# Displaced 5x5 depthwise convolution after a group norm: TensorE's loop rotated, fewer waits, a PSUM lane moved to VectorE, and a store issued earlier

## The chip, the cores and the metric

The kernel runs on one core of one Trainium2 chip. The metric is device time in microseconds (us) of one execution; the value of a kernel is the median of several. Besides, one execution was profiled, and all rows below are from that one. TensorE (PE, its weight loads PEld), VectorE (DVE), ScalarE (ACT), GpSimd (POOL) and SyncE (SP) run their own instruction streams and meet at semaphores. A `q` behind an engine's name means its sequencer, which waits, branches and issues DMAs.

## What is computed

The input `x` is float32, 32 x 384 x 64 x 64. It is group-normalised (32 groups of 12 channels), each block of 8 channels is displaced by a whole offset and convolved with a 5x5 Gaussian whose centre is moved by the offset's fraction, and the result is added to `x`:

```python
def _gn(v, G=32, eps=1e-5):
    g = v.reshape(B_, G, C_ // G, H_, W_)
    m = jnp.mean(g, axis=(2, 3, 4), keepdims=True)
    s = jnp.var(g, axis=(2, 3, 4), keepdims=True)
    return ((g - m) / jnp.sqrt(s + eps)).reshape(v.shape)

off_round = jnp.round(offset)                       # offset: 48 positions x (x, y)
disp = _displace(x.reshape(B, P, cpp, h, w), off_int)   # zero outside the image
sub = offset - off_round
d = field[None] + sub[:, None, None, :]
kernel = jnp.exp(-jnp.sum(d * d, axis=-1) / (2.0 * SIGMA ** 2))
kernel = kernel / jnp.sum(kernel, axis=(1, 2), keepdims=True)
out = lax.conv_general_dilated(disp, kw, padding=[(c, c), (c, c)], feature_group_count=C, ...)
x = x + out                                          # of _gn(x)
```

## The kernel before

The convolution is separable, so it is done as two matrix products with band matrices that hold displacement and kernel at once: `ay` for the image's rows and `ax` for its columns.

**Tiles.** The channels are cut into 16 superblocks (`NSUPER`) of 24 channels, the batch into 16 steps (`STEPS`) of two images, which makes 256 steps (`TOTAL`). A step is one slot of `xin`, [128 partitions, 6 channels, 256 elements], 786 KB; there are 16 slots, so each superblock reuses them all. SyncE loads a slot with two DMAs of 384 KB as soon as it has been stored, and ScalarE's sequencer issues the stores, two DMAs each. Four steps make a round (`QUAD`), four rounds a superblock.

**A step on TensorE** has two stages.
- The first stage (`y_product` for three positions, L722 to L729) multiplies the normalised input `norm` with `ay`: 48 products in four row strips of the array. It fills 384 columns of four PSUM banks, `ps[:, v]`. Even steps of a round write half `v` = 0, odd steps half 1. `norm` has two buffers, too, by the step's parity.
- The result is copied from PSUM to `y` (four buffers), one per lane (= bank): `copy_y` on ScalarE (L628), four lanes, and for the last step of a round three lanes, with the fourth copied by VectorE in `copy_last_lane` (L519).
- The second stage (`x_products`, L731) multiplies `y` with `ax` and writes the same PSUM half as the first stage of that parity. VectorE adds two thirds of the result to `xin` (`add_x`, L525); ScalarE copies the other third to `x2` (`copy_third`, L647) and GpSimd adds that (`add_third`, L329). Then the step can be stored.

Between the first stages stand the sums of the group statistics over the partitions, `sum_stats`, 8 small products with `ones`. VectorE makes the statistics themselves (`statistics`, three chunks a step, some five steps ahead), GpSimd turns them into scale and bias (`make_summands`, `coefficients`), and VectorE reads the sums out of PSUM for it (`sums`, L509).

**Normalising** a step is split: half of the channels on ScalarE (L617), half on GpSimd (L334). It can start when the first stage two steps earlier is done (`y_done`), because it overwrites that step's `norm`.

**TensorE's loop** (L825 to L830) runs once a round: an inner loop over the two pairs of `first_stages` (L765), then `second_stages` (L781). The pair before the loop stands apart, so that the inner loop has one pass in the first round. A pair is an even step, `sum_stats`, an odd step. `first_stages` waits before the even step for `x2_ready`, `result1_ready` and `y_ready`, and `y_even` for `norm0_ready`, `half0_ready` and `mats_ready[0]`. Semaphores that TensorE reads count steps, some with a head start of `SPARE` = 2. `second_stages` waits for `ax_ready`, `sums_ready` and the copies of the steps.

**ScalarE's order in a round** (L659 to L701), for steps 0 to 3 of the round: store 0 of the round before, `copy_y` 0, normalise 2, `copy_y` 1, store 1, normalise 3, `copy_y` 2, store 2, `copy_y` 3, store 3, `copy_third` 0, normalise 4, `copy_third` 1, `copy_third` 2, normalise 5, `copy_third` 3. Between superblocks `fill_rows` writes new rows of `ay`. This order is written out by hand, and so are VectorE's (12 statistics, a part of the matrices, `sums`, `copy_last_lane`, four `add_x`) and GpSimd's. A sequencer goes through its instructions in order: what stands behind a DMA issue is not started until the issue is through.

**The first round** of TensorE's loop runs code that is fetched for the first time, and the last four slots (`FIRST` = 12 on) are loaded only after `y_done` has reached 3.

## Time and profile before

| | us |
|---|---|
| median of 3 runs | 1219.58 (1217.87 to 1221.5) |
| the profiled execution, its own time | 1220.7 |
| its span, first to last instruction | 1218.6 |
| TensorE busy | 1157.7 (95%) |
| VectorE busy | 904.9 (74%) |
| GpSimd busy | 823.1 (68%) |
| ScalarE busy | 805.3 (66%) |
| moved between HBM and the core | 402.97 MB |

The span is from the first to the last instruction; the profiled execution's own time is 2.1 us longer. Busy counts neither register, branch and semaphore instructions nor DMA issues. Matmuls overlap in the array, so "busy" on PE is not "at its peak", and a gap on PE or PEld of 0.3 us between two stages is real idle time. In the rows, `[0.60 <-issue]` behind an instruction is the idle time of its engine before it and what ended it; `issue` means nothing that the profile shows. One round of TensorE in the rows is: 96 records of line 726 (a first stage), 8 of line 713 (`sum_stats`), 192 of line 726 (two first stages), 8 of line 713, 96 of line 726, 384 of line 738 (four second stages).

### The profile page before, as it was taken

The numbers are of one execution on the slowest core, as the hardware profiler recorded it, in microseconds if no ns is written. First come the engines' busy times: TensorE is split into PE (matmuls) and PEld (weight loads), VectorE is DVE, ScalarE is ACT, GpSimd is POOL, SyncE is SP. The second block draws the span as 40 slices with busy tenths as digits, with TensorE's granted clock in tenths as the row PEclk, the third lists the DMA queues.
The fourth block names the chain that finished last, engine by engine and source line by source line (L and its number), as shares of the span: only waits on it lengthen the run. The fifth ranks groups of instructions, "written<-read, shape, count | busy, mean of one in ns | idle before, by whom it ended". The sixth has DMA issues, their size and how long they took to land.

```text
span 1218.6 us, 112942 instructions
## 1 busy us (share of the span) xinstructions
PE 1157.7 (95%) x50408; PEld 1127.7 (93%) x50408; DVE 904.9 (74%) x1245; ACT 805.3 (66%) x874; POOL 823.1 (68%) x1176
## 2 busy tenths in 40 slices
PE   7699999999999999999999999999999999999996
PEld 7699999999999999999999999999999999999996
DVE  8467877777877868877777877778778777777762
ACT  4376676666676666676666666666676666676664
POOL 7466766776766866766766766767667666766764
PEclk9899999999999999999999999999999999999999
DMA  9499999999999999999999999999999999999966
GB/s 309 162 320 328 352 342 340 346 345 337 350 340 340 348 341 337 348 341 339 349 346 332 354 337 344 348 341 337 352 338 341 344 341 348 342 342 348 350 221 207
DMA packets 409762, 402.97 MB, mean 331 GB/s; under 512 B 16528, under 2 KB 409744, under 8 KB 409744
## 3 DMA queue, kind: packets, MB, share of 16 engines
q1 hardware_dynamic: 204944, 201.41, 50.2%
q10 hardware_dynamic: 204800, 201.36, 49.6%
q8 instruction: 7, 0.11, 0.0%
q14 instruction: 11, 0.09, 0.0%
HBM read 201.38 MB, written 201.33 MB: 330 GB/s over the span
## 4 chain that ended last, share of the span: by engine, by line
PE 83%; ACT 6%; issue 6%; ACTq 2%; POOL 1%; POOLq 0%; DVE 0%
PE ps L726 60%; PE ps L738 21%; ACT norm L623 4%; PE ps L713 2%; ACT x L651 2%; ACTq L657 2%; ACT ay L612 1%; POOL t_int L245 0%; ACTq L648 0%; POOL grid_i L225 0%; ACTq L650 0%; POOL t_full L252 0%; POOLq L54 0%; POOL grid L239 0%; POOL xin L332 0%
## 5 line engine op out<-in xcount | busy, mean ns | idle before, releaser
L726 PE MATMUL ps<-ay,norm 32*128 32x128 f32 x24576 | 755.9, 274 | 36.1 <-ACT norm L623 28.5
L726 PEld LDWEIGHTS ps<-ay,norm 32*128 32x128 f32 x24576 | 721.8, 188 | 54.2 <-issue 53.6
L634 ACT ACTIVATE y<-ps 128x1536 f32<-128x1536 f32 (+1 forms) x256 | 351.0, 1371 | 296.3 <-PE ps L713 184.8
L498 DVE BATCH_NORM_STATS2 stats<-xin 128x6 f32<-128x512 f32 x768 | 470.8, 691 | 0.1
L738 PE MATMUL ps<-ax,y 64*64 64x64 f32 x24576 | 391.2, 220 | 8.3 <-issue 7.1
L738 PEld LDWEIGHTS ps<-ax,y 64*64 64x64 f32 x24576 | 379.2, 135 | 19.4 <-issue 9.5
L528 DVE TENSOR_TENSOR xin<-ps,xin 128x1024 f32<-128x1024 f32 x256 | 313.5, 1225 | 83.9 <-PE ps L738 83.8
L332 POOL TENSOR_TENSOR xin<-x,xin 128x512 f32<-128x512 f32 x256 | 322.3, 1281 | 12.9 <-ACT x L651 12.6
L341 POOL TENSOR_SCALAR norm<-xin,rstd,bias 128x768 f32<-128x768 f32 x256 | 252.0, 987 | 113.2 <-issue 90.3
L623 ACT ACTIVATE norm<-xin,bias,rstd 128x768 f32<-128x768 f32 x256 | 262.0, 1024 | 23.6 <-issue 13.3
L651 ACT ACTIVATE x<-ps 128x512 f32<-128x512 f32 x256 | 150.7, 589 | 63.0 <-PE ps L738 60.8
L314 POOL TENSOR_TENSOR mean_sq<-both 128x8 f32<-128x8 f32 (+1 forms) x65 | 13.0, 200 | 223.7 <-DVE both L514 221.7
L514 DVE TENSOR_REDUCE both<-ps 128x24 f32<-128x288 f32 x63 | 28.8, 458 | 155.1 <-ACT y L634 155.1
L324 POOL TENSOR_TENSOR rstd<-var,mhalf 128x8 f32<-128x8 f32 (+1 forms) x65 | 106.7, 1642 | 5.1
L521 DVE COPY y<-ps 128x384 f32<-128x384 f32 x64 | 35.7, 558 | 61.5 <-PE ps L726 61.5
L713 PE MATMUL ps<-summands,ones 32*128 32x72 f32 (+1 forms) x1032 | 50.7, 251 | 1.2 <-POOL summands L295 1.2
L713 PEld LDWEIGHTS ps<-summands,ones 32*128 32x128 f32 x1032 | 45.2, 189 | 2.0 <-issue 0.9
L612 ACT ACTIVATE ay<-t_msk,same 128x256 f32<-128x256 f32 x48 | 23.7, 533 | 13.6 <-issue 11.6
L295 POOL TENSOR_TENSOR summands<-stats 128x24 f32<-128x24 f32 (+1 forms) x65 | 22.3, 343 | 9.8 <-POOL summands L293 9.7
L483 DVE SCALAR_TENSOR_TENSOR t_msk<-t_isq,t_exp 128x960 f32<-128x960 f32 x16 | 18.4, 1151 | 0.0
L460 DVE TENSOR_TENSOR t_full<-t_int,sub 128x960 f32<-128x960 f32 x15 | 17.8, 1186 | 0.0
L321 POOL TENSOR_TENSOR var<-spread,mean_sq 128x8 f32<-128x8 f32 (+1 forms) x65 | 14.0, 215 | 5.2 <-POOL spread L319 0.2
(63 smaller groups left out, 211.8 us busy)
## 6 DMA issues: line engine op xcount, KB each, us to landing
xin<-in_x_dram SPq DMA_DIRECT2D x512, 384.0 KB, 5.5
out_dram<-xin ACTq DMA_DIRECT2D x512, 384.0 KB, 5.3
off<-in_L_conv_offset_dram SPq DMA_DIRECT2D x1, 48.0 KB, 3.2
```

The source lines that it names most:

```text
L324: pool.tensor_tensor(rstd[:, v, part], var[:, v, part], mhalf[:, part], ALU.pow).then_inc(small, 1)
L332: pool.tensor_tensor(at, x2[:, s % QUAD], at, ALU.add).then_inc(result0_ready, 1)
L341: pool.tensor_scalar(norm[:, s % 2, :, cols].rearrange("p r (q w) -> p q r w", w=HW), xin[:, s, QG:].rearrange("p q (r w) -> p q r w", w=H ...
L498: nc.vector.bn_stats(stats[:, s // QUAD % 2, s % QUAD, n, :], xin[:, s].rearrange("p (g q) f -> p q f g", g=GROUPS)[:, n]).then_inc(bn_don ...
L528: nc.vector.tensor_tensor(at, ps[:, s % 2, 0:2].rearrange("p h (k f) -> p h k f", k=2), at, ALU.add).then_inc(result1_ready, 1)
L612: filled_k = nc.scalar.activation(ay[:, k].rearrange("p r (m b) -> p (r m) b", b=B)[:, :, part], t_msk[:, k, 0:R].rearrange("p r m -> p (r ...
L623: nc.scalar.activation(norm[:, s % 2, :, cols].rearrange("p r (q w) -> p q r w", w=HW), xin[:, s, 0:QG].rearrange("p q (r w) -> p q r w", ...
L634: nc.scalar.activation(y[:, j].rearrange("p k r a m -> p a (k r) m")[:, 0:lanes], ps[:, j % 2, 0:lanes, 0:POS * P].rearrange("p a (n m) -> ...
L651: nc.scalar.activation(x2[:, s % QUAD], ps[:, s % 2, 2:4, 0:ROW], ACT.Copy).then_inc(x2_ready, 1)
L713: last = nc.tensor.matmul(ps[:, v, a, place], ones[rows, :], summands[rows, part].rearrange("p t n s -> p (t n s)"), start=True, stop=True)
L726: last = nc.tensor.matmul(ps[:, v, a, P * k:P * (k + 1)], norm[rows, v, r, P * k:P * (k + 1)], ay[rows, k, r, :], start=(r == 0), stop=(r ...
L738: last = nc.tensor.matmul(ps[outs, v, 2 * (k // 2) + h, at:at + HW], y[rows, j, k, r].rearrange("p a m -> p (a m)")[:, outs], ax[rows, k], ...
```

## The change

- `second_stages` of a round comes first in TensorE's loop, then the first stages of the next round. The first stages of steps 2 and 3 stand before the loop. In the last pass the inner loop still makes one pair of first stages, for steps that don't exist; ScalarE and GpSimd raise the semaphores for it at their ends.
- Waits go: `y_ready` before both stages of a pair, `half0_ready` and `mats_ready[0]` before an even step, `ax_ready` and `y_ready` before the second stages. ScalarE waits for `half0_ready` at a superblock's border instead.
- VectorE copies the fourth lane of steps 0 and 1 of a round, too, between its statistics (after 3 and after 7 of the 12), and ScalarE's copies of those steps have three lanes. ScalarE waits for VectorE's copy before it normalises steps 2 and 3.
- Statistics run 17 chunks ahead, not 15, and `sums` stands before the making of the matrices.
- On ScalarE the store of step 3 of the round before is issued before `copy_y` 3, not behind it; `copy_third` 1 comes before normalise 4, and `copy_third` 2 before the second part of `fill_rows`.
- Slots 12 to 15 are first loaded when `x_done` has reached 4.

```diff
-AHEAD = QUAD + 1
+AHEAD = 17
...
-                    sync.wait_ge(y_done, 3)
+                    sync.wait_ge(x_done, ADDS * PAIR)
...
+            pool.engine_nop().then_inc(norm1_ready, PAIR)
+            pool.wait_ge(mats_ready[POS - 1], TOTAL)
+            pool.engine_nop().then_inc(mats_ready[POS - 1], 1)
...
-                dve.wait_ge(y_ready, evicted + 1 + SPARE)
+                dve.wait_ge(y_ready, evicted + 1)
...
-            def copy_last_lane(t):
+            def copy_last_lane(t, j):
+
                 dve.wait_ge(y_done, t + 1)
-                nc.vector.tensor_copy(y[:, QUAD - 1].rearrange("p k r a m -> p a (k r) m")[:, LANES - 1],
-                                      ps[:, 1, LANES - 1, 0:POS * P].rearrange("p (n m) -> p n m", m=32)
-                                      ).then_inc(last_lane_ready, QUAD)
+                nc.vector.tensor_copy(y[:, j].rearrange("p k r a m -> p a (k r) m")[:, LANES - 1],
+                                      ps[:, j % 2, LANES - 1, 0:POS * P].rearrange("p (n m) -> p n m", m=32)
+                                      ).then_inc(last_lane_ready, 1 + j // (QUAD - 1))
...
-            nc.vector.engine_nop().then_inc(y_ready, SPARE)
...
+            for part in range(AHEAD - CHUNKS * (QUAD + 1)):
+                statistics(0, QUAD + 1, part)
...
-                for f in range(s + AHEAD, s + AHEAD + QUAD):
+                for m in range(QUAD * CHUNKS):
+
+                    if m == 3:
+                        copy_last_lane(t, 0)
+                    if m == 7:
+                        copy_last_lane(t + 1, 1)
+                    f, part = divmod(CHUNKS * s + AHEAD + m, CHUNKS)
                     if f >= STEPS and not group_follows:
                         continue
...
-                    all_statistics(c + f // STEPS, f % STEPS)
+                    statistics(c + f // STEPS, f % STEPS, part)
+                if last:
+
+                    dve.wait_ge(y_ready, t + 3)
+                    nc.vector.engine_nop().then_inc(sums_ready, QUAD)
+                else:
+                    sums(quad + 1, (g + 1) % 2, t + 2, read=not first)
...
-                copy_last_lane(t + 3)
+                copy_last_lane(t + 3, QUAD - 1)
...
                 act.wait_ge(made, c + 1)
+                if k == 0:
+
+                    act.wait_ge(half0_ready, STEPS * (c + 1))
...
-                lanes = LANES - j // (QUAD - 1)
+                lanes = LANES if j == 2 else LANES - 1
...
                 copy_y(t, 0, first)
+                act.wait_ge(last_lane_ready, t + 1)
                 normalise(t + 2, s + 2, quad, first)
                 copy_y(t + 1, 1, first)
                 store_of_last_round(1)
+                act.wait_ge(last_lane_ready, t + 2)
                 normalise(t + 3, s + 3, quad, first)
                 copy_y(t + 2, 2, first)
                 store_of_last_round(2)
+                store_of_last_round(3)
                 copy_y(t + 3, 3, first)
-                store_of_last_round(3)
...
                 copy_third(t, s, first)
+                copy_third(t + 1, s + 1, first)
                 if not last:
                     normalise(t + 4, (s + 4) % STEPS, quad + 1)
-                copy_third(t + 1, s + 1, first)
+                copy_third(t + 2, s + 2, first)
                 if border:
                     fill_rows(c + 1, 1)
-                copy_third(t + 2, s + 2, first)
...
+            act.wait_ge(norm0_ready, TOTAL)
+            act.sem_inc(norm0_ready, PAIR)
+            act.wait_ge(mats_ready[1], TOTAL)
+            act.sem_inc(mats_ready[1], 1)
...
                 pe.wait_ge(norm0_ready, number)
-                pe.wait_ge(half0_ready, number)
-                pe.wait_ge(mats_ready[0], number)
                 y_product(0, 0)
...
-                after = pe.snap(number + 1)
                 pe.wait_ge(x2_ready, one)
                 pe.wait_ge(result1_ready, one)
-                pe.wait_ge(y_ready, number)
                 y_even(number)
                 pe.wait_ge(summands_ready, number)
                 sum_stats(0)
-                second = pe.snap(one + 1)
+                second, after = pe.snap(one + 1), pe.snap(number + 1)
                 pe.wait_ge(x2_ready, second)
                 pe.wait_ge(result1_ready, second)
-                pe.wait_ge(y_ready, after)
                 y_odd(after)
...
             def second_stages(one):
-                pe.wait_ge(ax_ready, one)
+
+
                 pe.wait_ge(sums_ready, one)
-                pe.wait_ge(y_ready, pe.snap(one + 4))
                 pe.sem_inc(x_started, 1)
                 x_products(0)
-                pe.wait_ge(last_lane_ready, one)
-                pe.wait_ge(y_ready, pe.snap(one + 5))
+                three = pe.snap(one + 3)
+                pe.wait_ge(last_lane_ready, three)
+                pe.wait_ge(y_ready, three)
...
-            begin = pe.alloc_register("begin")
-            pe.reg_mov(begin, 1 + PAIR)
+            y_even(3)
+            pe.wait_ge(summands_ready, 3)
+            sum_stats(0)
+            y_odd(4)
             with pe.Fori(1, TOTAL + 1, QUAD) as one:
-                end = pe.snap(one + QUAD)
-                with pe.Fori(begin, end, PAIR) as number:
-                    first_stages(one, number)
-                pe.reg_mov(begin, end)
                 second_stages(one)
+
+                following = pe.snap(one + QUAD)
+                end = pe.alloc_register("end")
+                pe.reg_alu(end, pe.snap(one + 2 * QUAD), TOTAL + 1 + PAIR, ALU.min)
+                with pe.Fori(following, end, PAIR) as number:
+                    first_stages(following, number)
```

## Rows read from the trace of the kernel before

**Rows 1.** The page: busy us of each engine; what the DMA queues moved.
```profile
PE 1157.7 (95%) x50408; PEld 1127.7 (93%) x50408; DVE 904.9 (74%) x1245; ACT 805.3 (66%) x874; POOL 823.1 (68%) x1176
...
DMA packets 409762, 402.97 MB, mean 331 GB/s; under 512 B 16528, under 2 KB 409744, under 8 KB 409744
```

**Rows 2.** Timeline of PE: start us, us, what, count [idle before], second and last rounds.
```profile
72.29 2.96 PE L726 MATMUL ps<-ay,norm 32*128 32x128 f32 x96 [0.46 <-ACT norm L623]
...
1190.80 2.96 PE L726 MATMUL ps<-ay,norm 32*128 32x128 f32 x96 [0.49 <-ACT norm L623]
...
1202.56 5.87 PE L738 MATMUL ps<-ax,y 64*64 64x64 f32 x384
```

**Rows 3.** Timeline of all engines, one round, from its second first stage on.
```profile
627.10 1.02 ACT L623 ACTIVATE norm<-xin,bias,rstd 128x768 f32<-128x768 f32 x1
...
628.44 2.80 PEld L726 LDWEIGHTS ps<-ay,norm 32*128 32x128 f32 x96 [0.29 <-issue]
628.48 1.45 ACT L634 ACTIVATE y<-ps 128x1536 f32<-128x1536 f32 x1 [0.36 <-PE ps L726]
...
628.69 1.39 ACTq L657 DMA_DIRECT2D out_dram<-xin  x2
...
630.18 1.03 ACT L623 ACTIVATE norm<-xin,bias,rstd 128x768 f32<-128x768 f32 x1 [0.25 <-issue]
...
631.34 2.81 PEld L726 LDWEIGHTS ps<-ay,norm 32*128 32x128 f32 x96
...
631.75 1.45 ACT L634 ACTIVATE y<-ps 128x1536 f32<-128x1536 f32 x1 [0.54 <-PE ps L713]
631.96 1.39 ACTq L657 DMA_DIRECT2D out_dram<-xin  x2
...
634.27 5.95 PE L738 MATMUL ps<-ax,y 64*64 64x64 f32 x371
...
634.48 1.13 ACT L634 ACTIVATE y<-ps 128x1152 f32<-128x1152 f32 x1 [1.28 <-PE ps L726]
...
634.68 1.50 ACTq L657 DMA_DIRECT2D out_dram<-xin  x2
...
636.34 0.60 ACT L651 ACTIVATE x<-ps 128x512 f32<-128x512 f32 x1 [0.74 <-PE ps L738]
```

**Rows 4.** Timeline of PEld: the first weight load of the next round.
```profile
640.85 1.33 PEld L726 LDWEIGHTS ps<-ay,norm 32*128 32x128 f32 x42 [0.60 <-issue]
```

**Rows 5.** TensorE's sequencer before it: duration ns min/median/max, first and last start us.
```profile
L825 PEldq ALU_OP  x1: 32/32/32, 640.0 to 640.0; - x1
L825 PEldq COMPARE_BRANCH  x1: 214/214/214, 640.1 to 640.1; - x1
...
L745 PEldq EVENT_SEMAPHORE  x1: 51/51/51, 640.5 to 640.5; - x1
```

**Rows 6.** Groups by line and shape: busy us, mean ns of one, idle before.
```profile
L498 DVE BATCH_NORM_STATS2 stats<-xin 128x6 f32<-128x512 f32 x768 | 470.8, 691 | 0.1
...
L634 ACT ACTIVATE y<-ps 128x1152 f32<-128x1152 f32 x64 | 72.3, 1130 | 83.3 <-PE ps L726 83.3
...
L521 DVE COPY y<-ps 128x384 f32<-128x384 f32 x64 | 35.7, 558 | 61.5 <-PE ps L726 61.5
```

**Rows 7.** Store issues at the end, columns as rows 5: the third, the other five.
```profile
L657 ACTq DMA_DIRECT2D out_dram<-xin x1: 608/608/608, 1208.6 to 1208.6; - x1
...
L657 ACTq DMA_DIRECT2D out_dram<-xin x5: 1022/1046/1117, 1209.2 to 1213.7; - x5
```

**Rows 8.** Windows: busy us by engine (PE, PEld, DVE, ACT, POOL), PEclk, DMA, GB/s.
```profile
622.48:640.88 18.40, 17.78 (x784) 17.39 (x785) 14.28 (x20) 11.91 (x14) 13.58 (x20) 1.00 1.03 344
...
1209.00:1218.60 9.60, 0.00 (x0) 0.00 (x0) 0.24 (x1) 0.13 (x1) 1.29 (x2) 0.71 0.91 308
```

**Rows 9.** Timeline of the first round's second stages and the next round's begin.
```profile
42.77 3.37 PE L738 MATMUL ps<-ax,y 64*64 64x64 f32 x127 [3.89 <-issue]
...
52.38 4.59 PE L726 MATMUL ps<-ay,norm 32*128 32x128 f32 x96 [0.56 <-issue]
```

More of the change, by code:

```diff
@@ L570, in one_round @@
                         values(c + 1)
-                if last:
-                    nc.vector.engine_nop().then_inc(sums_ready, QUAD)
-                else:
-                    sums(quad + 1, (g + 1) % 2, t + 2, read=not first)
-                copy_last_lane(t + 3)
+                copy_last_lane(t + 3, QUAD - 1)
                 if g == ROUNDS - 1 and group_follows:
@@ L796, in second_stages @@
                 x_products(2)
-                three = pe.snap(one + 3)
                 pe.wait_ge(x2_ready, three)
```

2 lines of the change are left out of this document (1 added, 1 removed).

## Prediction

> **What bounds the kernel now.** I read the page's busy shares first. TensorE is busy for 1157.7 of 1218.6 us and no other engine for more than 905 [rows 1], so the time is TensorE's order of work plus its gaps. Next the period. From the round at 72.29 to the one at 1190.80 us there are 61 rounds, so one takes 18.34 us [rows 2]. There are 63 such rounds after the slow first one, and whatever is won or lost in a round counts 63 times. Then one round in order of time [rows 3]: two pairs of first stages, then four second stages. The gaps sit at the joints. TensorE's weight loads stand idle for 0.29 us before the second pair begins at 628.44, and for 0.60 us between the second stages and the next round [rows 3, 4]. Within the second stages 5.95 us stand for 384 matmuls, against 5.87 in the last round, where nothing follows [rows 2, 3].
>
> Last, the chain through ScalarE, whose sequencer issues the stores between the instructions that TensorE needs. The copy of step 1's result starts at 628.48. Its store issue runs from 628.69 to 630.08, the normalising that waits behind it starts at 630.18 and ends at 631.21, and TensorE begins step 3 at 631.34, 0.13 later [rows 3]. The copy of step 3 runs from 634.48 to 635.61, and since the second stage of step 1 writes the same PSUM half, it cannot start before. The second stage of step 0 started at 634.27 and needs about 5.87/4 = 1.47 us, so it is done at 635.74. That copy is on time by 0.1 us and no more.
>
> **The change part by part.** A round is taken as its times in rows 3, and each part shifts them.
>
> *Order and length of the PE loop.* The order of the matmuls is the same: what was done at the loop's head is done before the loop for steps 2 and 3, and at its foot for the next round. What moves is the loop's own instructions. Before, the joint from second to first stages holds add, branch, two register operations and three waits: from the add at 640.0 to the first weight load at 640.85, of which the branch and what follows it take 0.3 us [rows 4, 5]. After, the branch lies behind first stages, where the sequencer runs ahead (there the weight loads begin 0.29 late only because of ScalarE, or at once). In its place come one or two additions and a minimum, some 0.1 us each by the spacing of those rows, and two of the three semaphore instructions go. 0.85 becomes about 0.55, a gain of 0.30 us (bounds 0.15 and 0.45). At the joint from first to second stages the branch costs 0 to 0.1; I take 0.03 and count it in the 0.30.
>
> *First pair to second pair.* VectorE takes a lane of step 0, so ScalarE's copy falls from 1.45 to 1.13 us [rows 3, 6], and the normalising that ended at 628.12 ends at 627.80. TensorE came 0.32 after it, behind two more semaphore instructions that go away. Both together exceed the gap, so the 0.29 us is gone: the second pair starts at 628.15. The new wait stands on ScalarE, ahead of the normalising, and behind it queue everything of the round. It is met: VectorE's lane takes 0.56 us against 1.13 of ScalarE's [rows 6], if it begins with it. VectorE has three statistics of 0.69 us before it [rows 6] and the whole first stage of step 0 for them, 2.96 us [rows 2], since the copy starts only when that is through. If it came late, each 0.1 us beyond the slack of 0.57 (1.13 less 0.56) would be lost in every round.
>
> *Second pair, step 3.* Here the gain is lost again. The normalising for step 3 started 1.70 us after the copy did, because 1.39 us of store issue lie between, not because of the copy, which ended at 629.93. The copy of step 1 waits for step 1, which has not moved. So step 3 begins at about 631.34 as before, and so does the second stage of step 0 at 634.27. VectorE's second lane buys nothing.
>
> *The store of step 3 ahead of the copy of step 3.* This decides. The copy of step 2 starts 0.29 earlier, at 631.46. Its store's issue ends 1.60 us after (631.75 to 633.35 now), at 633.06. The next store starts 0.21 later, at 633.27, takes D, and then about 0.2 us to the copy's start (its own wait is long met): 633.47 + D, against 634.48. The copy is late by D - 1.01, and it was just in time, so the second stages wait for all of it. For D the nearest rows are: 1.39 us for a pair of issues with room before it, 1.50 for this store now, though it follows the last by 1.33 us [rows 3]. When stores follow each other at once, at the kernel's end, the third issue took 0.61 and the fourth to eighth 1.02 to 1.12 us each [rows 7]. A pair that stands third and fourth would be 0.61 + 0.16 + 1.02 = 1.79. I take D = 1.60, between 1.50 and 1.79, since four issues in a row are only just the number at which it began. So +0.59 us a round; bounds +0.38 (D = 1.39) and +1.09 (D = 2.10, both issues near 1.0).
>
> The Trainium skill (Perfetto Trace Analysis, DMA Instruction — HWDGE) says that an issue's profiled time includes waiting for a descriptor generator that another sequencer may hold locked. By it one load issue in the way would add some 0.6 us, so D would be 2.0 and the kernel near 1261 us. The trace neither shows nor excludes it.
>
> *Copies of the third rows.* The copy at 636.34 started only when the store's issue had ended at 636.18 [rows 3]; that store is now elsewhere, and the copy of step 1 no longer stands behind a normalising of 1.03 us. This takes the second stages from 5.95 to about 5.87 us and something more in the border rounds: 0.10 us a round (0.05 to 0.20). The normalising moved back is due 2 us later, so nothing is late for it.
>
> *VectorE's order.* Two copies of 0.56 us a round are added to 14.28 busy of 18.40 [rows 8], with room. The statistics go two chunks further ahead before the loop, which hides them. The distances and values now stand behind the sums; nothing on the path asks for them.
>
> *Head.* The first pass through new code stalls TensorE, once for 3.89 us [rows 9], while the loads of the last four slots are in flight. They now start after two second stages, which takes away up to 3 us. Steps 2 and 3 have code of their own now, so the loop's first stages are fetched later, for one to two more stalls of up to 3. I take +0.5 (bounds -3 and +6).
>
> *Tail.* The loop now ends with one pair of first stages on no data, and their release is ScalarE's, behind its last store issue, which starts at 1213.7 and takes 1.12 [rows 7]: 1214.8. TensorE has then been idle for 6 us and its clock is down: 0.71 granted on average over the last 9.6 us, so part of it at 1.2 GHz [rows 8]. A first stage at such a start took 4.59 us against 2.96 [rows 2, 9]. So 1214.9 + 4.6 + 0.2 + 2.9 = 1222.6, and 0.4 to the end, against 1218.6: +4.5 us (2.8 at full clock, 7 if both steps are slow).
>
> **The sum.** 0.59 - 0.30 - 0.10 = +0.19 us a round, times 63 = +12.0; with the head 0.5 and the tail 4.5, +17 us. The profiled execution took 1220.7 us (span 1218.6 and 2.1 around it): 1237.7. It stands 1.1 above the median of 1219.58, so 1236.6, and I say 1236.
>
> **The rivals.**
> - *The gains and the late copy cancel* (0.18). D stays at 1.39 to 1.45, since the store issue of this kernel seldom backs up while the loads share the engines. Then -0.02 to +0.04 a round, and with the tail 1216 to 1225. For it: most pairs of issues are 1.39. Against: the tail's fourth issue.
> - *Back-pressure* (0.13). D reaches 2.1: 1.09 - 0.40 = +0.69 a round, 43 us, near 1265; above D of about 1.8 the kernel leaves my case.
> - *Faster* (0.14). The copy of step 3 isn't late, because the two stores' issues are through before step 3 ends or my spacing between them is too wide, while every shorter joint holds: 0.30 + 0.10 + 0.29 = 0.69 us a round, 43 us, less the tail: near 1182. It needs step 3 to begin 0.29 earlier too, and the row of the store issue before its normalising speaks against that. With only the joint and the thirds won it is 0.40 x 63 - 5 = 20 us, near 1200. The point from which it decides: a copy that starts later than 634.3 in this round's time undoes it. The Trainium skill (SBUF — State Buffer, A bandwidth-pool intuition that's wrong) gives about 358 GB/s between HBM and one core. The trace moves 344 over a round [rows 8], and 402.97 MB in 64 rounds at 358 would hold a round at 17.6 us, which is where this rival ends, so it would not go below.
> - *The change doesn't do what it says* (0.05). The removed waits were merged into instructions that remain, so the joints stay as long as they are, and only the late copy counts: 0.59 x 63 + 5 = 42, near 1262.
>
> **How the numbers follow.** My case has 0.50 and spreads over D from 1.45 to 1.8 and the joint's bounds: 1222 to 1252. Faster by over 0.3% (below 1216): 0.14 and a third of the cancelling case, 0.20. Within 0.3%, which is about what a measurement of this kernel can tell from no change: most of the rest of that case and the low edge of mine, 0.15. Slower: 0.65. The range is 1204 to 1258: it leaves out most of the faster case and the top of the back-pressure.
>
> **What would show it.** Right: ScalarE's queue shows four issues in a row of 3.2 to 3.4 us in each round, the copy of 128x1152 starts right behind them, and TensorE waits inside the second stages for that copy, 0.5 to 0.7 us a round, as a new row of the waits. The joint to the first stages falls from 0.60 to about 0.3, the one between the pairs vanishes, step 3's normalising still ends 2.7 us after the copy starts, and the round is 18.5 us. At the end stand 192 matmuls of first stages from 1.2 GHz on. Wrong: a copy that starts within 0.1 us of step 3's end, or a pair of issues that stays at 1.39.

## The result, and the profile after

The changed kernel takes 1247.48 us (median of 4 runs, 1246.37 to 1250.61), against 1219.55 us for the kernel before (median of 4 runs) on the same chip: the ratio is 1.0233, with a 95% interval of 1.0208 to 1.0258. It is slower by 27.9 us; 16.5 were forecast. The profiled execution has a span of 1244.5 us and its own time is 1246.4.

The page of the kernel after: engine shares, bandwidth, and two waits out of its list.

```profile
PE 1155.9 (93%) x50608; PEld 1130.8 (91%) x50608; DVE 968.7 (78%) x1373; ACT 750.7 (60%) x874; POOL 853.0 (69%) x1176
...
HBM read 201.38 MB, written 201.33 MB: 324 GB/s over the span
...
PEld ps L762 <- issue: 77.0, 94, 4.4
...
ACT y L651 <- PE ps L762: 156.9, 53, 3.6
```

Against [rows 1] TensorE does 192 matmuls more (the pair on no data) and is busy for 1.8 us less, while the span is 25.9 us longer. So the loss is idle time. The new waits are on the second stages, now line 762: their weight loads stand idle 94 times for 77 us in total. "Issue" means that the profile shows no releaser, so the cause has to be read from the order of events. First the period: these two rows answer [rows 2].

```profile
70.39 2.38 PE L750 MATMUL ps<-ay,norm 32*128 32x128 f32 x73
...
1212.62 2.96 PE L750 MATMUL ps<-ay,norm 32*128 32x128 f32 x96
```

There are 61 rounds between them, so a round takes 18.73 us, where it took 18.34. (The row at 72.29 in [rows 2] and the one at 70.39 here begin the third of the 64 rounds, not the second, which begins at 52.38 [rows 9].) One round in order of time, TensorE and ScalarE, which answers [rows 3]. Line 750 is a first stage, 737 the sums, 762 a second stage, 651 `copy_y`, 640 the normalising, 668 `copy_third`, 674 a store's issue.

```profile
640.96 1.13 ACT L651 ACTIVATE y<-ps 128x1152 f32<-128x1152 f32 x1 [0.68 <-PE ps L750]
641.07 0.54 DVE L526 COPY y<-ps 128x384 f32<-128x384 f32 x1
641.17 1.39 ACTq L674 DMA_DIRECT2D out_dram<-xin  x2
...
642.68 1.03 ACT L640 ACTIVATE norm<-xin,bias,rstd 128x768 f32<-128x768 f32 x1 [0.59 <-issue]
...
643.76 2.96 PE L750 MATMUL ps<-ay,norm 32*128 32x128 f32 x96
643.82 1.45 ACT L651 ACTIVATE y<-ps 128x1536 f32<-128x1536 f32 x1
644.02 4.12 ACTq L674 DMA_DIRECT2D out_dram<-xin  x4
...
646.74 1.63 PE L762 MATMUL ps<-ax,y 64*64 64x64 f32 x96
...
648.33 1.13 ACT L651 ACTIVATE y<-ps 128x1152 f32<-128x1152 f32 x1 [3.06 <-PE ps L762]
...
649.56 4.43 PE L762 MATMUL ps<-ax,y 64*64 64x64 f32 x288 [1.20 <-issue]
...
653.92 2.96 PE L750 MATMUL ps<-ay,norm 32*128 32x128 f32 x96
```

Four store issues in a row last from 644.02 to 648.14. The copy of step 3 starts behind them at 648.33, though TensorE had finished step 3 at about 646.7. It ends at 649.46, and 0.10 later TensorE goes on, having been idle for 1.20 us. This is the step that the prediction called decisive. Its size is different: 4.12 us for the four issues, where 3.2 to 3.4 were forecast (on average over the rounds they take 4.02). The profile names "PE ps L762" as what the copy waited for. That is only the semaphore that came last; what held it was its own sequencer.

Two other places are as described or better. The second stages go over to the next round at 653.92 with no idle time in brackets (0.60 before, [rows 4]), and between the pairs nothing is idle any more. Step 3 still waits for a normalising that stands behind a store issue (642.68 to 643.71, TensorE at 643.76).

The end of the kernel, TensorE and ScalarE's queue:

```profile
1230.55 6.21 ACTq L674 DMA_DIRECT2D out_dram<-xin  x6
...
1236.96 4.30 PE L750 MATMUL ps<-ay,norm 32*128 32x128 f32 x96 [6.60 <-ACTq L724]
1241.08 0.36 PE L737 MATMUL ps<-summands,ones 32*128 32x72 f32 x8
1241.26 2.91 PE L750 MATMUL ps<-ay,norm 32*128 32x128 f32 x96
```

The pair on no data starts when ScalarE's last six issues are through. TensorE had been idle for 6.60 us by then and the first step takes 4.30 us instead of 2.96. The window of these stages (us, busy time of PE, PEld, DVE, ACT, POOL, granted clock, DMA share, GB/s) has a granted clock of 0.74, so part of it ran at 1.2 GHz:

```profile
1235.00:1244.40 9.40, 7.21 (x200) 7.05 (x200) 0.00 (x0) 0.00 (x0) 0.00 (x0) 0.74 0.49 167
```

To compare kernels I took from each trace the mean distance between the first weight loads of successive stages, over the 62 rounds from the third on. S0 to S3 are the first stages, X0 to X3 the second stages of a round. The row "by matmuls" has the distance from S3 to X0 between their first matmuls instead. D is the time from the start of the first to the end of the second issue of the store of step 3, over the rounds in which loads still run (the stores of rounds 3 to 58).

```
us              before  after    E1    E2    E4    E5    E6    E8    E7   E10   E12
S0 to S1          2.90   2.90  2.90  2.90  2.90  2.90  2.90  2.90  2.90  2.90  2.90
S1 to S2          3.04   2.68  2.69  3.04  3.06  2.68  2.68  2.84  2.69  2.79  2.68
S2 to S3          2.93   3.14  3.15  2.90  2.90  3.13  3.14  2.98  2.91  2.95  3.06
S3 to X0          2.92   2.91  2.91  2.92  3.12  2.91  2.92  2.91  2.93  2.91  2.92
  by matmuls      2.87   3.07  3.08  2.86  3.09  3.05  3.06  3.14  2.98  3.03  3.00
X0 to X1          1.41   2.69  1.54  2.68  1.40  1.88  1.98  1.61  1.48  1.54  1.51
X1 to X2          1.53   1.39  1.55  1.39  1.46  1.39  1.40  1.56  1.93  1.40  1.40
X2 to X3          1.50   1.40  1.40  1.41  1.42  1.40  1.40  1.40  1.39  1.44  1.42
last load of X3
 to next S0       0.70   0.20  0.20  0.69  0.37  0.20  0.20  0.20  0.20  0.20  0.20
round            18.34  18.73 17.75 19.34 18.02 17.89 18.01 17.80 17.83 17.52 17.48
D                 1.51   2.32  1.67  2.04  1.54  1.48  1.61  1.76  2.13  1.42  1.41
```

The two rows for S3 to X0 differ in the kernels with the rotated loop. In the kernel after, in E1 and in E10 the first weight load of X0 is issued in time, but the second follows only 0.17 to 0.18 us later, and with it the first matmul (0.04 in E4, 0.01 in the kernel before). Two lines of E1:

```profile
614.63 0.13 PEld L762 LDWEIGHTS ps<-ax,y 64*64 64x64 f32 x1
614.92 5.69 PEld L762 LDWEIGHTS ps<-ax,y 64*64 64x64 f32 x383 [0.16 <-issue]
```

So about 0.2 us a round that belongs to the joint from first to second stages stands in the row X0 to X1 (in E4 in S3 to X0).

### The profile page after: what moved, and what is told of

Read it like the earlier page. It is cut to its first block and busy times, and to the rows that moved or that the text cites. A ratio compares the mean times of both kernels' runs of the same rounds, so it can differ in the third digit from the quotient of the medians.

```text
span 1244.5 us, 113105 instructions
## 1 busy us (share of the span) xinstructions
PE 1155.9 (93%) x50608; PEld 1130.8 (91%) x50608; DVE 968.7 (78%) x1373; ACT 750.7 (60%) x874; POOL 853.0 (69%) x1176
## 5 line engine op out<-in xcount | busy, mean ns | idle before, releaser
L651 ACT ACTIVATE y<-ps 128x1152 f32<-128x1152 f32 (+1 forms) x256 | 310.1, 1211 | 349.5 <-PE ps L762 156.9
L502 DVE BATCH_NORM_STATS2 stats<-xin 128x6 f32<-128x512 f32 x768 | 482.5, 693 | 0.0
L762 PEld LDWEIGHTS ps<-ax,y 64*64 64x64 f32 x24576 | 379.2, 135 | 84.6 <-issue 77.0
L762 PE MATMUL ps<-ax,y 64*64 64x64 f32 x24576 | 388.3, 219 | 72.2 <-issue 69.0
L314 POOL TENSOR_TENSOR mean_sq<-both 128x8 f32<-128x8 f32 (+1 forms) x65 | 50.9, 784 | 207.9 <-DVE both L518 205.9
L526 DVE COPY y<-ps 128x384 f32<-128x384 f32 x192 | 106.2, 553 | 65.1 <-PE ps L737 40.6
L737 PE MATMUL ps<-summands,ones 32*128 32x72 f32 (+1 forms) x1040 | 47.8, 250 | 1.0 <-POOL summands L295 1.0
L295 POOL TENSOR_TENSOR summands<-stats 128x24 f32<-128x24 f32 (+1 forms) x65 | 15.0, 230 | 9.8 <-POOL summands L293 9.7
L319 POOL TENSOR_TENSOR spread<-inner,both 128x8 f32<-128x8 f32 (+1 forms) x65 | 13.8, 213 | 5.4
```

The costliest lines, as they stand in the source:

```text
L502: nc.vector.bn_stats(stats[:, s // QUAD % 2, s % QUAD, n, :], xin[:, s].rearrange("p (g q) f -> p q f g", g=GROUPS)[:, n]).then_inc(bn_don ...
L526: nc.vector.tensor_copy(y[:, j].rearrange("p k r a m -> p a (k r) m")[:, LANES - 1], ps[:, j % 2, LANES - 1, 0:POS * P].rearrange("p (n m) ...
L651: nc.scalar.activation(y[:, j].rearrange("p k r a m -> p a (k r) m")[:, 0:lanes], ps[:, j % 2, 0:lanes, 0:POS * P].rearrange("p a (n m) -> ...
L737: last = nc.tensor.matmul(ps[:, v, a, place], ones[rows, :], summands[rows, part].rearrange("p t n s -> p (t n s)"), start=True, stop=True)
L762: last = nc.tensor.matmul(ps[outs, v, 2 * (k // 2) + h, at:at + HW], y[rows, j, k, r].rearrange("p a m -> p (a m)")[:, outs], ax[rows, k], ...
```

## The experiments

The theory after the result: the store of step 3 ahead of the copy costs more than everything else gains, and apart from it the change makes the kernel faster. The rivals: the new waits and lanes cost the time, or the gains are limited by the transfers anyway.

**E1, the store behind the copy again.** All of the change but this:

```diff
                 store_of_last_round(2)
-                store_of_last_round(3)
                 copy_y(t + 3, 3, first)
+                store_of_last_round(3)
```

> The changed kernel, but the store of step 3 is issued behind the copy of step 3 again, as in the kernel before. Theory (the two store issues in a row hold that copy back, 2.69 us between the second stages of steps 0 and 1 where 1.40 are needed): that gap falls to 1.40, all other joints stay as in the changed kernel, so the round is 18.73 - 1.29 = 17.44 us and the time 1247.5 - 62 x 1.29 = about 1167 us. Rival (the transfers bind as soon as TensorE's order doesn't: the rate over a round would have to be 361 GB/s, and the highest of the page's slices after the change are 350): the round stays near 18.0 us, 1247.5 - 62 x 0.73 = about 1202 us, and TensorE or VectorE shows waits for loads or stores. Rival (the joint itself is slower, not the copy): no change from 1247 us.

Measured: 1186.96 us, ratio to before 0.9733 (0.971 to 0.9757). So one line in the order turns a loss of 2.3% into a gain of 2.7%; its own share is 60.5 us, 0.98 us a round. The round of 17.75 us lies between the 17.44 of the theory and the 18.0 of the rival: the forecast of 1167 was too good. The copies of the thirds stand behind a store issue again (X1 to X2 1.55 for 1.39), and X0 to X1 is 1.54, not 1.40. The trace of E1, from the copy of step 3 on:

```profile
632.41 1.13 ACT L651 ACTIVATE y<-ps 128x1152 f32<-128x1152 f32 x1 [1.50 <-PE ps L750]
632.43 5.83 PE L762 MATMUL ps<-ax,y 64*64 64x64 f32 x384
632.60 1.60 ACTq L674 DMA_DIRECT2D out_dram<-xin  x2
```

The copy starts with the second stages, and these run through: 5.83 us for 384 matmuls. The 1.55 us from X1 to X2 are a mean: in the rounds before a superblock's border it is 1.80 us, because `fill_rows` stands there as well, and in some others the store's issue is longer (D goes up to 2.28). The 1.54 from X0 to X1 are not the copy's: in every round it starts 0.08 to 0.21 us behind the first weight load of X0, as in the kernel before (0.13 to 0.21). They are the late second weight load shown above; between first matmuls X0 to X1 is 1.41 us.

**E2, the move of the store alone**, in the kernel before, the same two lines:

> The kernel before with one part of the change: the store of step 3 is issued ahead of the copy of step 3. Theory: the pair of issues takes 2.3 us as in the changed kernel, the copy starts 1.60 + 0.21 + 2.3 + 0.2 = 4.3 us after the copy of step 2 where it started 2.75 after, so 1.55 us late; some 0.15 comes back from the thirds; 1.4 x 62 = 87 us slower, about 1306 us. Rival (the long issues come from the shorter round, more bytes a us, and not from four issues in a row): the pair stays near 1.6, the copy is 0.85 late, 0.7 x 62 = 43 us, about 1263 us.

Measured: 1286.54 us, ratio 1.056 (1.0538 to 1.0581). D is 2.04 us and X0 to X1 2.68, and the round is 19.34. With E1 this shows the mechanism from both sides. The forecast of 1306 took D from the kernel after (2.32) and was too high; the result lies halfway between it and the rival's 1263. So both have a part in the long pair of the kernel after: the four issues in a row (1.51 to 2.04 with nothing else changed) and the rest of the change, with its shorter round (2.04 to 2.32). One round of E2:

```profile
641.03 1.45 ACT L634 ACTIVATE y<-ps 128x1536 f32<-128x1536 f32 x1 [0.48 <-PE ps L713]
641.22 3.72 ACTq L657 DMA_DIRECT2D out_dram<-xin  x4
645.10 1.13 ACT L634 ACTIVATE y<-ps 128x1152 f32<-128x1152 f32 x1 [2.62 <-PE ps L738]
```

**E4, the rotated loop alone**, in the kernel before, with the pair on no data and all waits kept:

```diff
-            begin = pe.alloc_register("begin")
-            pe.reg_mov(begin, 1 + PAIR)
+            first_stages(1, 3)
             with pe.Fori(1, TOTAL + 1, QUAD) as one:
-                end = pe.snap(one + QUAD)
-                with pe.Fori(begin, end, PAIR) as number:
-                    first_stages(one, number)
-                pe.reg_mov(begin, end)
                 second_stages(one)
+
+                following = pe.snap(one + QUAD)
+                end = pe.alloc_register("end")
+                pe.reg_alu(end, pe.snap(one + 2 * QUAD), TOTAL + 1 + PAIR, ALU.min)
+                with pe.Fori(following, end, PAIR) as number:
+                    first_stages(following, number)
```

> The kernel before with the rotated loop of TensorE alone, extra pair at the end included; all waits stay, no lane moves, the stores stay. Theory (the branch and the loop's registers are what the joint from second to first stages is made of): 0.70 us from the last weight load of a round to the next falls to about 0.40; 0.3 x 62 = 19 us less, 4 us more at the end, about 1205 us. Rival (the joint is made of waits): it stays near 0.65, and with the end 1219 to 1223 us. In both the joint between the two pairs stays at 3.04 us, since it hangs on ScalarE's copy and normalising.

Measured: 1204.58 us, ratio 0.9888 (0.9866 to 0.991). The time is the expected one, but it comes about otherwise. The joint to the first stages falls from 0.70 to 0.37, as expected, and 0.20 of that is lost at the other joint, where the branch now stands (S3 to X0 is 3.12 us for 2.92 by weight loads, 3.09 for 2.87 by matmuls). What makes up for it is 0.15 from X1 to X3, perhaps because the second stages start later against ScalarE's order and find more of its copies done; that isn't shown. The kernel after doesn't have the kept waits, and its joints are 0.20 by weight loads and 3.07 by matmuls. So the removed waits bring about another 0.17 at the joint to the first stages and next to nothing at the other. No run takes out the waits alone.

**E5 and E6, why the issues last so long.** Both are the changed kernel with one thing left out, so that their output isn't the asked one. E5 leaves out the loads of superblocks 2 to 16; the statistics wait for the store of the slot instead. E6 keeps every load and its number of pieces, but each piece is a quarter as wide. E6's edit:

```diff
-            def load(c, s):
+            THIN = ROW // 4
+
+            def load(c, s, wide=ROW):
                 for b in range(B):
-                    sync.dma_start(xin[b:P:B, s], x_t[s, b, c]).then_inc(loaded[s], 16)
+                    sync.dma_start(xin[b:P:B, s, :, 0:wide], x_t[s, b, c][:, :, 0:wide]).then_inc(loaded[s], 16)
...
                 for s in range(SLOTS):
                     sync.wait_ge(stored[s], 16 * B * c)
-                    load(c, s)
+                    load(c, s, THIN)
```

> The changed kernel without the loads of superblocks 2 to 16: every slot is loaded once, the rest computes on what lies there, and VectorE's statistics wait for the store of the slot instead of its load. It leaves out 189 MB of loads. Theory A (a store issue is long when ScalarE's own queue is full, and loads matter only as they slow its draining): the pair of the store of step 3 stays long, 1.8 us or more as in the kernel's end, the gap between the second stages of steps 0 and 1 at 2.1 or more, the time above 1210 us. Theory B (issues hold each other up, the generator is shared with SyncE's loads): with no loads issued the pair falls to 1.39, the gap to 1.75, the round to 17.8 and the time to 1190 us or less.

> The changed kernel with loads of a quarter of the width from superblock 2 on: as many load issues with as many pieces (384 of 256 B instead of 1024 B), 25% of the bytes; the other three quarters of a slot keep what was there. Theory (a store issue is long when the queue of stores drains slowly beside the loads' bytes): the pair of the store of step 3 falls from 2.32 us to 1.5, as without loads, the gap between the second stages of steps 0 and 1 from 2.69 to about 1.9, the time to about 1200 us. Rival (the load issues themselves are in the way): pair and gap stay, 1240 us or more.

Measured: E5 1196.21 us, ratio 0.9825 (0.9804 to 0.9845), with D at 1.48. E6 1204.46 us, ratio 0.9873 (0.9856 to 0.9891), with D at 1.61. The four issues of one round in E5 and in E6:

```profile
632.78 3.12 ACTq L673 DMA_DIRECT2D out_dram<-xin  x4
```

```profile
637.97 3.13 ACTq L676 DMA_DIRECT2D out_dram<-xin  x4
```

E5 comes out near the numbers of theory B (pair 1.39, round 17.8, 1190 us) and far from those of theory A, but E6 speaks against B's reason: with as many load issues as before but a quarter of their bytes, most of the excess is gone. So what makes a store issue long here is the loads' bytes under way, and not the number of load issues beside it. The last rounds of the kernel after say the same with nothing left out. Its last load issue is at 1180 us; from then on the four store issues of a round take 3.12 to 3.13 us, about as in E5 (3.14 on average), against 4.02 on average in the rounds before:

```profile
1186.14 3.12 ACTq L674 DMA_DIRECT2D out_dram<-xin  x4
```

The total is the same although there the two issues of a store follow each other at 0.03 us (D is 1.74 then) and in E5 at 0.16 us (D is 1.48). So D alone depends on the spacing, too, and the length of all four is the better measure.

I counted the store issues of the kernel after between 100 and 1150 us by how many store issues had started in the 3.2 us before each, and by whether a load issue ran at the same time. With none or one before it, an issue beside a load issue takes 0.62 to 0.63 us on average (120 of them, at most 0.75); the median of all its store issues is 0.62. With two before it, the 101 issues beside which no load issue ran take 0.78 on average and up to 1.30, and in E5 none of that kind takes more than 0.65. With three before it, 49 ran beside a load issue and take 1.25 on average, at most 2.05; the 6 others take 0.95. In E5 the fourth of a row takes 0.72 us on average. The prediction weighed the rule of the Trainium skill (Perfetto Trace Analysis, DMA Instruction — HWDGE) that an issue also waits for a generator which another sequencer holds. By it D would have been 2.0, near the measured 2.32. But a load issue beside a lone store issue doesn't lengthen it, and store issues get long with no load issue beside them, so that rule alone doesn't explain the excess. 1.25 against 0.95 for the fourth leaves room for a share of it, but a long issue also has more time to meet a load issue.

What E5 and E6 don't tell is whether the issue waits for the queue's own earlier stores or for room that all queues share. The kernel after had both, four stores in a row and the loads beside them.

**E8, VectorE's new lanes left out of E1.** ScalarE copies four lanes of steps 0 and 1 again.

```diff
-                lanes = LANES if j == 2 else LANES - 1
+                lanes = LANES - j // (QUAD - 1)
...
-                    if m == 3:
-                        copy_last_lane(t, 0)
-                    if m == 7:
-                        copy_last_lane(t + 1, 1)
...
-                act.wait_ge(last_lane_ready, t + 1)
...
-                act.wait_ge(last_lane_ready, t + 2)
```

> The run with the store of step 3 behind the copy, without VectorE's copies of a lane of steps 0 and 1 (ScalarE copies all four, 1.45 us). Theory (since TensorE comes 0.05 us after what it waits for, where it was 0.33 before, the waits taken out were worth about as much as the lane): step 1 to step 2 is 0.33 + 1.35 + 1.02 + 0.05 = 2.75 us instead of 2.69, step 3 doesn't move as it hangs on the store issue; 0 to 0.1 us a round, 1187 to 1193 us. Rival (the lane made the gain, as I had it in the prediction): 3.0 us, 0.3 x 62 = 19 us, about 1206 us.

Measured: 1190.61 us, ratio 0.9761 (0.9742 to 0.9781), against 0.9733 for E1: the lanes are worth about 0.05 us a round (17.80 for 17.75), and the intervals overlap. S1 to S2 is longer without them (2.84 for 2.69) and S2 to S3 shorter by about as much (2.98 for 3.15). What VectorE's lane gives to step 2, the store issue ahead of the normalising takes from step 3.

**E7, E10, E11 and E12, the other stores.** If a store issue ahead of work that TensorE needs costs time, the others do too. E7 is E1 with the store of step 1 behind the normalising of step 3:

```diff
-                store_of_last_round(1)
                 act.wait_ge(last_lane_ready, t + 2)
                 normalise(t + 3, s + 3, quad, first)
+                store_of_last_round(1)
```

> The run with the store of step 3 behind the copy, and the store of step 1 behind the normalising of step 3, too. Theory (ScalarE's queue sets the start of step 3: 1.70 us from the copy of step 1 to the normalising, of which the copy needs 1.13): step 2 to step 3 falls from 3.15 to 2.90 us, the round from 17.75 to 17.50, 0.25 x 62 = 15 us less, about 1171 us, at 360 GB/s over a round. Rival (the transfers are the bound from about 355 GB/s on): the gain is given back by waits for stores or longer issues, 1180 to 1187 us.

Measured: 1192.21 us, ratio 0.9762 (0.974 to 0.9783), no better than E1. S2 to S3 falls from 3.15 to 2.91, as meant, and X1 to X2 rises from 1.55 to 1.93:

```profile
633.94 1.54 ACTq L674 DMA_DIRECT2D out_dram<-xin  x2
...
636.67 2.55 ACTq L674 DMA_DIRECT2D out_dram<-xin  x2
...
639.38 1.08 ACT L668 ACTIVATE x<-ps 128x512 f32<-128x512 f32 x2 [1.77 <-PE ps L762]
...
640.12 3.03 PE L762 MATMUL ps<-ax,y 64*64 64x64 f32 x192 [0.67 <-ACT x L668]
```

Three stores now stand close together, the last pair takes 2.55 us, and the copies of the thirds behind it come late. The lateness has moved to another place. The rival named longer issues, too, but ascribed them to a bound of the transfers from about 355 GB/s on; E10, below, averages 358 and is faster.

E10 is E7 with the store of step 3 behind the first copy of a third, and with ScalarE's releases for the pair on no data ahead of the last three stores:

```diff
                 copy_y(t + 3, 3, first)
-                store_of_last_round(3)
...
                 copy_third(t, s, first)
+                store_of_last_round(3)
                 copy_third(t + 1, s + 1, first)
...
                 if last:
+                    act.wait_ge(norm0_ready, TOTAL)
+                    act.sem_inc(norm0_ready, PAIR)
+                    act.wait_ge(mats_ready[1], TOTAL)
+                    act.sem_inc(mats_ready[1], 1)
                     for j in range(1, QUAD):
                         store(c, s + j, t + j)
             run(one_round)
...
-            act.wait_ge(norm0_ready, TOTAL)
-            act.sem_inc(norm0_ready, PAIR)
-            act.wait_ge(mats_ready[1], TOTAL)
-            act.sem_inc(mats_ready[1], 1)
```

> The store of step 1 behind the normalising of step 3, the store of step 3 behind the first copy of thirds, and at the end ScalarE raises the semaphores of the extra pair before its last three stores. Theory: as the run with the store of step 1 moved (about 1171 us), and the border rounds lose their 0.3 us before the second stage of step 2 (16 x 0.3 = 5 us less); at the end TensorE's extra pair runs beside the stores, so that from the last second stage to the end it is 10.4 us as before the change instead of 14.4: about 1162 us. Rival (transfers bound): 1175 us and more, with the end still 4 us shorter.

Measured: 1167.57 us, ratio 0.9569 (0.9552 to 0.9586). The round is 17.52 us, and from the last load of the second stages to the end it takes 10.45 us instead of 14.4, so the tail's 4 us are gone as well. Rows of E10's end, and three windows, two of one round each and one of 1000 us (us, then busy time of PE, PEld, DVE, ACT, POOL, granted clock, DMA share, GB/s):

```profile
1155.59 1.17 PE L749 MATMUL ps<-ay,norm 32*128 32x128 f32 x32 [0.30 <-ACTq L720]
1155.67 6.03 ACTq L674 DMA_DIRECT2D out_dram<-xin  x6
```

```profile
629.73:647.10 17.37, 17.21 (x791) 17.08 (x785) 14.23 (x21) 11.56 (x14) 12.97 (x18) 1.00 1.05 354
647.10:664.50 17.40, 17.30 (x794) 17.17 (x788) 15.55 (x23) 12.20 (x16) 12.23 (x19) 1.00 1.07 365
...
100.00:1100.00 1000.00, 989.22 (x44732) 978.51 (x44725) 855.69 (x1197) 666.14 (x771) 751.26 (x1015) 1.00 1.06 358
```

TensorE is busy for 17.21 of 17.37 us of a round: here it is the bound. The transfers run at 358 GB/s on average, 343 in the same window of the kernel before, and no engine's waits name a load of `xin`: so the rival that they limit the gains isn't borne out up to this rate. What is left stands in the first round of a superblock, which takes 17.96 us against 17.37 in the others. Two more runs tried small things on E10: E11 loads slots 12 to 15 already when `y_done` is 3, as the kernel before does, and E12 puts the store of step 0 behind the normalising of step 2 in those first rounds.

```diff
-                    sync.wait_ge(x_done, ADDS * PAIR)
+                    sync.wait_ge(y_done, 3)
```

> The fastest run so far (stores of steps 1 and 3 moved, the extra pair released earlier) with the last four slots loaded from y_done 3 on, as in the kernel before. Theory (the loads delay the fetch of code that TensorE runs for the first time): the first round's stall in the second stages grows again by some 2 to 3 us, the second round begins at 71 to 72 us instead of 69.3, the time is 2 to 3 us longer. Rival (the later loads bring nothing, the other parts of the change shorten the head): no change.

```diff
-                store_of_last_round(0)
+                if g:
+                    store_of_last_round(0)
                 copy_y(t, 0, first)
                 act.wait_ge(last_lane_ready, t + 1)
                 normalise(t + 2, s + 2, quad, first)
+                if not g:
+                    store_of_last_round(0)
```

> The fastest run so far, with the store of step 0 behind the normalising of step 2 in the first round of each superblock. There ScalarE's copy of step 0 waits 0.7 us behind a store that waits for GpSimd's addition, and the joints into steps 2 and 3 are 0.47 and 0.18 longer than in the other rounds. Theory: these rounds fall from 17.96 to about 17.4 us, 15 x 0.55 = 8 us less, about 1159 us. Rival (the store only moves its lateness, to the stores that follow or to VectorE's waits for a free slot): 1165 us or more.

Measured: E11 1166.71 us, ratio 0.9572 (0.9557 to 0.9587); E12 1167.22 us, ratio 0.9577 (0.9561 to 0.9592). Neither differs from E10. When the last slots are loaded doesn't matter: the delay that E11's theory forecast for the head isn't there. In E12, S1 to S2 of the first rounds falls from 3.15 to 2.68 us and S2 to S3 rises from 3.08 to 3.55, so those rounds stay at 17.96: the lateness moved once more. The trace shows where to. The list of waits of E12 has this row:

```profile
PEld ps L739 <- POOL summands L295: 7.3, 16, 0.6
```

Line 739 is `sum_stats`, which stands between S2 and S3. In all 15 such rounds of E10 and of E12 it begins 0.05 us behind GpSimd's `summands`, where these are ready 0.58 us before it in the other rounds. So there GpSimd's queue holds TensorE, and a store moved on ScalarE can't help. No run changes GpSimd's order, so what that would bring is open. The best versions, E10 to E12, are 4.3% faster than the kernel before and about 6.5% faster than the changed one.

## Why the prediction was right, and where its terms were off

The direction, the place and the order of size were right: the late copy outweighs the gains. The sum came out lower than the measurement by 11 us, out of errors that partly cancel, and that the time lies in the range is in part luck. With the measured D and the forecast gains, the prediction's own sum gives 0.91 us a round and about 1282 us, outside the range. The gains were 0.89 us a round instead of 0.40.

```
us a round                          forecast   measured
last second stage to first stages     -0.30      -0.50   (0.70 to 0.20)
step 1 to step 3                       0         -0.15   (5.97 to 5.82)
late copy of step 3 (X0 to X1)        +0.59      +1.28   (1.41 to 2.69)
copies of the thirds (X1 to X3)       -0.10      -0.24   (3.03 to 2.79)
sum                                   +0.19      +0.39   (18.34 to 18.73)
```

Over 61 rounds the measured sum is 23.7 us. The head gives 1.9 back (the third round starts at 70.39 instead of 72.26 us), and the tail costs 4.0 (14.4 us from the last load of the second stages to the end, 10.4 before): together 25.8, against 25.9 between the spans.

- **The late copy: the mechanism right, D mis-sized.** D was taken as 1.60 and is 2.32 us. The prediction read it from the kernel's end [rows 7], where the third and fourth issues took 0.61 and 1.02. In the rounds of the kernel after they take 0.95 and 1.21 on average. Part of the error was the row: at the end no loads are under way, and E5 and E6 show that loads with their bytes are what lengthens the issues. The other part was the choice of a value below what the row gave: it gave 1.79, and the kernel after has 1.74 in its last rounds, without loads. By its own formula, D - 1.01, the delay would have been 1.31 with the right D, and the measured rise of X0 to X1 is 1.28. D belongs to the back-pressure rival, which gave 2.1 and 1265 us (its own terms, 43 us for the rounds and 5 for head and tail, make 1268); the kernel isn't that slow because the gains were larger than forecast.
- **The joint to the first stages: half as much again.** 0.50 us went, where the bounds were 0.15 and 0.45. In the trace one addition, one register move and one semaphore instruction are left in the place of [rows 5]: they start at 653.5, 653.7 and 653.8, and the weight load at 653.92. The addition begins while the last second stage still runs, and the branch is no longer there. E4 shows that the rotation alone brings 0.33 at this joint and loses 0.20 at the other; the rest at this joint, 0.17, came with the waits gone. The prediction put the branch's cost at the other joint at 0 to 0.1, since "the sequencer runs ahead" there. That was wrong: between first matmuls, S3 to X0 is 2.87 us before and 3.07 after, 3.09 in E4. In the kernel after it costs nothing only because X1 waits for the late copy anyway; in E1 it does. The net of both joints is then 0.50 less 0.20, the forecast 0.30, by two errors that cancel.
- **Step 3 doesn't start earlier: nearly right.** S1 to S2 lost 0.36 and S2 to S3 took 0.21 back. The rest, 0.15, is the shorter lag from ScalarE's normalising to TensorE's step 3: 0.05 us, where it was 0.21 on average before (0.13 in the round that the prediction read). E8 has the same 5.82 us with neither of VectorE's lanes, so the statement that the second lane buys nothing holds, and E7 confirms that the store issue is what stood in the way.
- **The copies of the thirds: 0.24, above the bounds.** With the store elsewhere, X1 to X3 goes from 3.03 to 2.79 us. E2 has 1.39 and 1.41 for its two parts, so moving the store ahead of the copy is enough for the whole gain. I had read one round, in which 0.08 was lost; the mean over all rounds, with the border's 1.71 us for X1 to X2, was in the trace and would have said 0.24.
- **VectorE** had the room that was forecast: its lane (641.07) begins 0.11 after ScalarE's copy and ends 0.48 before it. The new wait on ScalarE isn't seen.
- **The head** gave 1.9 us, where +0.5 was forecast (bounds -3 and +6). What gave it is open, and it may be no gain at all. E4, which doesn't touch the last slots' loads, starts its third round at 70.40 us. But E2, which has the loop and the loads of the kernel before, starts it at 70.44, and the kernels that have the loop and the loads of the changed one (E1, E7, E8, E10, E12) start it between 69.26 and 71.50. With one profiled execution of each, 1.9 us can't be told from such differences.
- **The tail** came as forecast, 4.0 us for 4.5, and by the mechanism named: E10 raises the semaphores ahead of the stores and the 4 us are gone.
- **The rivals.** "Faster" is what E1 shows with the one line taken back: 1187 us, near the 1182 that this rival gave. Its point of decision, the start of the copy of step 3, was the right one. Its bound from the transfers, 17.6 us a round, isn't refuted: the Trainium skill (SBUF — State Buffer, A bandwidth-pool intuition that's wrong) gives about 358 GB/s between HBM and one core, and E10 moves 358 on average over 1000 us, 17.52 us a round. Single rounds go to either side, 354 and 365, so 358 isn't a hard limit for one round; whether more could be sustained, no run shows, since TensorE is the bound there.

## What to carry to other kernels

A DMA issue is an instruction of the engine that issues it. Before one is moved, ask what stands behind it in that sequencer and when TensorE needs it; put it where the engine has slack, and look again afterwards, for the lateness may just have moved to the next place (E7, E12). Price several issues in a row only from rows in which the queues are as loaded as they will be, never from the kernel's end. Measure a joint by the first matmul as well as by the first weight load, for a single load can run ahead. When a change bundles gains and one bad step, undo its parts one by one: here the change without one moved line gained more (2.7%) than it lost with it (2.3%).

## What the runs showed of the hardware

- A lone store issue of 384 KB takes 0.62 us, also beside a load issue. The third and fourth of a row take 0.95 and 1.21 us on average in the kernel after, up to 2.05, where 335 GB/s flow (100 to 1100 us). With nothing loaded, four in a row take 3.12 us from the first's start to the fourth's end, whether the fourth itself then takes 0.71 (E5's rounds) or 1.10 (the end of the kernel after).
- A core exchanged 358 GB/s with HBM over 1000 us (E10), 354 and 365 over two rounds of 17.4 us, and the page of E10 has 371 in one of its 40 slices.
- A loop's branch with its register work cost TensorE 0.33 us a round behind the second stages (0.70 us in the kernel before, 0.37 in E4) and 0.2 us behind the first stages (2.87 us from S3 to X0 by matmuls in the kernel before, 3.09 in E4, 3.07 in the kernel after). The branch itself lasts 0.21 us in [rows 5].
